# Cross-attention with image-prompt tokens: the output projection one step later with its halves in plain order, and each tile of x loaded in four parts

## What is computed

```python
q = heads(x @ W_q); k_t = heads(text @ W_k); v_t = heads(text @ W_v)
probs_t = softmax(q k_t^T * 32**-0.5)
text_out = probs_t @ v_t
sem = l2norm(probs_t @ text) @ l2norm(ip)^T
probs_ip = softmax(q k_ip^T * 32**-0.5 + 0.5 * sem) * spatial_mask
out = (text_out + probs_ip @ v_ip) @ W_out + b_out + x
```

## Time and profile before

| | |
|---|---|
| times of the kernel before | 1108.41, 1114.44, 1116.14 us (median 1114.44) |
| the profiled execution | 1114.77 us |
| its span from first to last instruction | 1112.9 us |
| granted TensorE clock, mean | 0.974 of full |
| TensorE busy | 92% of the span, over 97% in the middle of the main loop |
| VectorE busy | 76% |
| DMA engines' busy share | 77% |

### The profile page before, as it was taken

One profiled execution on the slowest core, in us unless ns is written; L12 is line 12 of the kernel. 1 busy time (PEld: TensorE's weight loads), 2 busy tenths in 40 slices (PEclk: granted clock), 3 DMA queues, 4 the chain that ended last, 5 costly groups with the idle time before them and its releaser, 6 DMA issues.

```text
span 1112.9 us, 23936 instructions
## 1 busy us (share of the span) xinstructions
PE 1026.0 (92%) x7829; PEld 839.5 (75%) x7829; DVE 840.6 (76%) x2400; ACT 676.1 (61%) x1979; POOL 575.0 (52%) x1535
## 2 busy tenths in 40 slices
PE   6994587899999999999999999999999999999978
PEld 5872466778787878787887878787878787877856
DVE  3145277888888888888888888788878888887862
ACT  1134376766676666766766766676776676676630
POOL 0000255655565665656555656565656656655650
PEclk9798798999999999999999999999999999999989
DMA  9498556877869887968879778878698778877662
GB/s 292 137 210 184 133 112 143 150 161 148 184 130 194 177 166 137 195 136 155 164 159 194 150 161 163 179 138 185 128 199 164 174 146 177 144 143 139 136 115 81
DMA packets 465941, 177.63 MB, mean 160 GB/s; under 512 B 433417, under 2 KB 442917, under 8 KB 465817
## 3 DMA queue, kind: packets, MB, share of 16 engines
q1 hardware_dynamic: 465817, 176.10, 76.6%
HBM read 43.15 MB, written 28.05 MB: 64 GB/s over the span
## 4 chain that ended last, share of the span: by engine, by line
PE 72%; DVE 9%; DMA 4%; issue 2%; POOL 2%; ACT 1%; SPq 1%; DVEq 0%; POOLq 0%
PE ps_O L1003 27%; PE ps_Q L1037 21%; PE ps_U L1023 11%; PE ps_S L979 10%; DMA pts<-ph 3%; PE ps_M L1051 2%; DVE pr L917 1%; DVE n L929 1%; DVE f L933 1%; DVE x_in L866 1%; DVE attn L942 1%; PE ps_M L1065 1%; DVE f L949 1%; DMA x_in<-in_x_dram 1%; ACT pr L770 1%
## 5 line engine op out<-in xcount | busy, mean ns | idle before, releaser
L770 ACT ACTIVATE pr<-ps_S,bias 128x73 f32<-128x73 f32 x1280 | 288.7, 338 | 171.9 <-DVE bias L881 171.9
L847 POOL TENSOR_TENSOR ph<-pr,ph 128x440 f16<-128x440 f32 x320 | 228.2, 734 | 241.2 <-ACT ph L782 241.0
L1003 PE MATMUL ps_O<-wo_hi,aT 128*128 128x320 f16 x1280 | 295.5, 302 | 25.2 <-DVE x_in L866 25.2
L1037 PE MATMUL ps_Q<-xT,wq_hi 128*128 128x512 f32 x800 | 279.7, 415 | 6.2 <-DVE qT L854 6.1
L782 ACT ACTIVATE ph<-pr 128x584 f16<-128x584 f32 x320 | 204.2, 688 | 7.6 <-DMA pts<-ph 2.6
L1003 PE MATMUL ps_O<-wo_lo,aT 128*128 128x320 f16 x640 | 192.2, 300 | 0.0
L1003 PEld LDWEIGHTS ps_O<-wo_hi,aT 128*128 128x128 f16 x1280 | 125.4, 98 | 86.8 <-DVE x_in L866 29.5
L1023 PE MATMUL ps_U<-xm,pts 128*128 128x110 f16 (+1 forms) x2560 | 158.7, 214 | 17.3 <-DMA pts<-ph 16.9
L979 PE MATMUL ps_S<-kbd,qT 128*128 128x308 f32 x960 | 171.0, 314 | 1.1 <-ACT pr L770 1.0
L1037 PEld LDWEIGHTS ps_Q<-xT,wq_hi 128*128 128x128 f32 x800 | 145.9, 190 | 33.5 <-DVE qT L854 8.0
L874 DVE TENSOR_REDUCE smax<-ps_S 128x8 f32<-128x584 f32 x160 | 121.9, 762 | 62.0 <-PE ps_S L979 61.6
(11 more groups left out here) (163 smaller groups left out, 1380.1 us busy)
## 6 DMA issues: line engine op xcount, KB each, us to landing
x_in<-in_x_dram SPq DMA_DIRECT2D x16, 1280.0 KB, 6.7
out_dram<-x_in SPq DMA_DIRECT2D x64, 320.0 KB, 3.1
w_k<-in_L_xattn_W_k_dram SPq DMA_DIRECT2D x5, 512.0 KB, 9.1
w_ip<-in_L_xattn_W_k_ip_dram SPq DMA_DIRECT2D x1, 2560.0 KB, 11.9
w_v<-in_L_xattn_W_v_dram SPq DMA_DIRECT2D x1, 2560.0 KB, 19.8
w_ip<-in_L_xattn_W_v_ip_dram SPq DMA_DIRECT2D x1, 2560.0 KB, 10.3
pts<-ph SPq DMA_TRANSPOSE x160, 4.4
xm<-x_d SPq DMA_DIRECT2D x20, 110.0 KB
```

The costliest lines, as they stand in the source:

```text
L770: last = nc.scalar.activation(pr[p % P_RING][:, j, h, :], sc[:, j, h, 0:T], ACT.Exp, bias=bias[p % 2][:, j, h:h + 1], scale=SCALE)
L847: nc.gpsimd.tensor_tensor(lo, full[:, :, t0:t1], one[:, :, 0, t0:t1], ALU.subtract).then_inc(pl_ready, 1)
L1003: last = nc.tensor.matmul(o_bank[half % 2][:, 0:HALF], stationary, moving, start=(k, a, b_) == O_MMS[0], stop=(k, a, b_) == O_MMS[-1])
L1037: last = nc.tensor.matmul(ps_Q[:], wq[a][:, c, k * P:(k + 1) * P], xT[(CC * i + c) % XT_RING][b_][:], start=(c, a, b_) == Q_MMS[0], stop=( ...
```

## The change

The output of a tile begins in step 6 instead of step 5 after the tile's ten steps, and its pieces go half by half; before, the third pieces of halves 0 and 1 stood together in step 7. The stores and the ring of steps move with it. The load of a tile of x becomes four loads of one subtile (320 KB each), one step after the store that frees the same subtile. In SyncE's order of a step the `pts` transposition now stands before the `aT` transposition, and the load of `vw_sb` is last.

```diff
-    FIRST, LAST = -4, STEPS * (TILES + 1) + 7
+    FIRST, LAST = -4, STEPS * (TILES + 1) + 8
-    OUT_AT = {5: ((0, 0), (0, 1)), 6: ((1, 0), (1, 1)), 7: ((0, 2), (1, 2)), 8: ((2, 0), (2, 1), (2, 2)),
-              9: ((3, 0), (3, 1), (3, 2)), 10: ((4, 0), (4, 1)), 11: ((4, 2), (5, 0)), 12: ((5, 1), (5, 2)),
-              13: ((6, 0), (6, 1), (6, 2)), 14: ((7, 0), (7, 1), (7, 2))}
-    STORE_AT = {9: 0, 11: 1, 14: 2, 16: 3}
+    OUT_AT = {6: ((0, 0), (0, 1)), 7: ((0, 2), (1, 0)), 8: ((1, 1), (1, 2)), 9: ((2, 0), (2, 1), (2, 2)),
+              10: ((3, 0), (3, 1)), 11: ((3, 2), (4, 0)), 12: ((4, 1), (4, 2)), 13: ((5, 0), (5, 1), (5, 2)),
+              14: ((6, 0), (6, 1), (6, 2)), 15: ((7, 0), (7, 1), (7, 2))}
+    OUT_FROM = min(OUT_AT)
+    STORE_AT = {10: 0, 13: 1, 15: 2, 17: 3}
+    LOAD_AT = (-19, -16, -14, -12)
...
                 for j in range(1, TILES):
-                    if p == max(STEPS * j - 13, FIRST):
-                        if j >= X_RING:
-                            sp.wait_ge(x_stored[j % X_RING], 16 * SUB * (j // X_RING))
-                        sp.dma_start(x_in[j % X_RING][:], rows(x, j)).then_inc(x_loaded[j % X_RING], 16)
+                    for q in range(SUB):
+                        if p == max(STEPS * j + LOAD_AT[q], FIRST):
+                            if j >= X_RING:
+                                sp.wait_ge(x_stored[j % X_RING], 16 * (SUB * (j // X_RING - 1) + q + 1))
+                            sp.dma_start(x_in[j % X_RING][:, q], rows(x, j)[:, q]).then_inc(x_loaded[j % X_RING], 16)
...
                     sp.dma_start_transpose(pts[p % PT_RING][:].rearrange("p j k c -> p (j k) c"),
                                            ph[p % PH_RING][:].rearrange("p j h k c -> p (j h k c)")
                                            ).then_inc(pts_loaded[p % PT_RING], 16)
+
+                m = slot_of(p - 5)
+                if m is not None:
+
+                    sp.wait_ge(at_hi, m + 1)
+                    sp.wait_ge(at_lo, m + 1)
+                    if m >= AT_RING:
+                        sp.wait_ge(o_ready, OUTS * ((m - AT_RING) // CC + 1))
+                    sp.dma_start_transpose(aT[m % AT_RING][:], at16[m % 2][:].rearrange("p k s c -> p (k s c)")
+                                           ).then_inc(aT_loaded[m % AT_RING], 16)
+                for b in range(B):
+                    if p == 2 * SLOTS * b + 15:
+
+                        if b:
+                            sp.wait_ge(o_ready, NI * OUTS * b)
+                        else:
+                            sp.dma_start(vw[IPR:IPR + 1].bitcast(F32), b_d).then_inc(vw_loaded, 16)
+                        sp.dma_start(vw[0:IPR].bitcast(F32), vw_d[b]).then_inc(vw_loaded, 16)
...
-                        pe.wait_ge(x_loaded[j % X_RING], 16 * (j // X_RING + 1))
+                        pe.wait_ge(x_loaded[j % X_RING], 16 * (SUB * (j // X_RING + 1) if j % X_RING else SUB * (j // X_RING) + 1))
```

More of the change, by code:

```diff
@@ L646, in out_at @@
     def out_at(p):
-        i, at = divmod(p - 5, STEPS)
-        return [(i - 1, half, piece) for half, piece in OUT_AT[at + 5]] if 0 <= i - 1 < TILES else []
+        i, at = divmod(p - OUT_FROM, STEPS)
+        return [(i - 1, half, piece) for half, piece in OUT_AT[at + OUT_FROM]] if 0 <= i - 1 < TILES else []
     def ip_at(p):
@@ L685, in _ @@
                                              x_d[b, tile, 0:n, c * HG:(c + 1) * HG, :]).then_inc(xm_loaded[c], 16)
[L686 to L692, removed]
+                for i in range(TILES):
+                    if p - STEPS * (i + 1) in STORE_AT:
+                        q = STORE_AT[p - STEPS * (i + 1)]
+                        sp.wait_ge(o_added, OUTS * i + 2 * q + 2)
+                        sp.dma_start(rows(out, i)[:, q], x_in[i % X_RING][:, q, :]).then_inc(x_stored[i % X_RING], 16)
+                for j in range(1, TILES):
+                    for q in range(SUB):
[3 more added lines that the diff above has]
+                            sp.dma_start(x_in[j % X_RING][:, q], rows(x, j)[:, q]).then_inc(x_loaded[j % X_RING], 16)
+                if pair_of(p) is not None:
+                    sp.wait_ge(ph_ready, p + 1)
+                    sp.wait_ge(pl_ready, 2 * (p + 1))
+                    if p >= PT_RING:
+                        sp.wait_ge(u_ready, p - PT_RING + 1)
+                    sp.dma_start_transpose(pts[p % PT_RING][:].rearrange("p j k c -> p (j k) c"),
+                                           ph[p % PH_RING][:].rearrange("p j h k c -> p (j h k c)")
+                                           ).then_inc(pts_loaded[p % PT_RING], 16)
                 m = slot_of(p - 5)
```

## The result

The change made the kernel faster by far less than forecast: 1110.22 us (median of 18 runs, 1101.65 to 1113.97) against 1113.43 (18 runs) for the kernel before, a ratio of 0.9962 with a 95% interval of 0.9948 to 0.9977. Measured again in experiment 1 it was 1109.69 against 1112.50, ratio 0.9969 (0.9950 to 0.9988). That is 3 us off instead of 18.6, and 1110 us lies outside the range of 1086 to 1105.

What follows compares the result with a forecast made beforehand. TensorE was taken to bound the loop, waiting nearly only for VectorE's addition. Terms -20.8 + 2.8 - 5.2 + 1.0 + 0.5 + 5.7 - 1.2 - 1.4 = -18.6 took 1114.77 to 1096 us; range 1086 to 1105.

Steps and rivals of the forecast that it cites:

- the term for `vw_sb`: Load now behind `pts` and `aT` makes TensorE wait in steps 17, 57, 97, 137: +3.0 and +2.7, together +5.7 us.
- The landing: Time from issue to landing of the 400 KB `vw_sb` load, taken as the 3.1 us of a 320 KB DMA.
- The wait in step 8: All 14 loop waits of TensorE for VectorE's addition of a finished half, in step 8 of ten, go: -20.8 us.
- what is late next: Exponentials before the next scores in shortened step 8, and `pts` before U: 0.2 per tile, 14 times, +2.8 us.
- Four loads for one: Load of x in parts: nothing in the loop; first steps -5.2 and +1.0; tile 1's load +0.5 us.
- the blocking rival: Load parts in steps 4, 6 and 8 delay `pts`, TensorE waits 7.8 us per tile: 1205 us, chance 0.05.
- All is hidden: Rival: the `vw_sb` load lands in time and step 8 loses nothing: 1088 us, chance 0.22.
- A new wait takes the place of the old one: Rival: `bias` or `pts`(8) 0.8 to 1.3 us late per tile, 11 to 18 come back: about 1108, chance 0.17.
- Both ends: Step 15, losing 12 output matmuls, counted -1.2 us; the drain counted -1.4 us (from -4 to +2.5).
- The drain's reason: The 2.35 us wait and some 3.8 of VectorE's lateness go, against 2.4 of added matmul work: -1.4 us.

Runs made afterwards that it cites:

- experiment 1: The changed kernel run again unchanged for a second profile, beside the kernel before: 1109.69 us, ratio 0.9969.
- kernel 8: Changed kernel with the `aT` transposition back ahead of the stores and the `vw_sb` load ahead of `pts`: 1091.01 us, repeated at 1091.82.
- kernel 4: Kernel before with only the load of x cut in four parts, output order and SyncE's order as before: 1111.11 us, ratio 0.9980.
- kernel 7: New output order alone: changed kernel with whole loads of x, `aT` at its old place and `vw_sb` ahead of `pts`: 1103.35 us, ratio 0.9907.
- kernel 2: Changed kernel with the `vw_sb` load issued ahead of `pts`, `aT` still behind it: 1095.12 us, repeated at 1092.27.
- kernel 3: Changed kernel with each tile of x loaded whole by one DMA of 1280 KB: 1123.18 us, ratio 1.0093.
- kernel 6: Changed kernel with the `vw_sb` load between `pts` and `aT` instead of behind both: 1098.27 us, ratio 0.9857.
- kernel 5: Kernel before with only SyncE's new order, `aT` behind `pts` and the `vw_sb` load last in its step: 1135.64 us, ratio 1.0200.

## Why the prediction was wrong, step by step

**The ledger of the runs.** New output order alone: -9.6 us (1103.35 against 1112.98). Loads in parts on top of it: -12.3 (1091.01). SyncE's new order on top of both: +18.7 (the changed kernel at 1109.69). Together -3.2, the result, as it must be, since each step is measured from the one before it; the last step crosses two groups of runs. The forecast had the first two right in sum (-24.3 without its term for `vw_sb`, measured -22.0 and -22.2 in the two comparisons of kernel 8) and the third at less than a third of its size. That the first two agree in sum is no proof of their parts: I had put 18.0 on the order and under 4 on the loads, and the order alone gave 9.6. What one is worth depends on the other, as experiments 4 and 7 show.

**The step that failed is the term for `vw_sb`**: +5.7 forecast, +14.6 measured against kernel 2 beside it, +17.4 against its repeat (on another chip). The place (steps 17, 57, 97, 137) was right, and for step 57 the issue time and the deadline to 0.3 us. Two sizes were off.

- *The landing.* I took 3.1 us, the median of a 320 KB store, for a load of 400 KB that stands behind two transposing DMAs and ahead of a load of x. It took 4.3 to 5.0. So the waits were 2.43, 1.93, 1.79 (forecast 1.0 each) and 4.98 (2.7): 11.1 instead of 5.7. Why it took longer is open. The load of x behind it is not the reason: in kernel 3 nothing follows it for 3.7 us in steps 55, 95 and 135, and it releases TensorE 5.0, 4.0 and 4.3 after its issue, against 4.9, 4.4 and 4.3 (rows below; only in step 15 is it 4.2 against 5.0). Nor is `aT` ahead of it alone: in kernel 6 `aT` stands behind it, and the four take 4.0 to 5.5. The bounds that I gave (0 to 9 and 0 to 5) held the waits, 6.2 and 5.0; with the clock behind it the first costs some 7.
- *The clock.* The sum had no term for it, though the trace of before had shown two stretches: one at the wait of 5.28 in its first steps, and one in its drain, behind the 2.35 of the earlier trace rows, where matmuls of O grew from 0.30 to 0.47. Behind some of the waits of 1.6 us and more, and all from 2.9 on, the granted clock was half for 3.4 or 6.8 us. In the changed kernel the three stretches of the loop cost 5.6 and 6.0 us of time in the two profiles (from the steps, as in experiment 5), 1.5 of it behind a `pts` wait; in kernel 5 it was 8.7 for four waits.

Kernel 3's queue and its wait in step 57, with S(55) at 452.41:

```profile
461.22 1.76 SPq L716 DMA_TRANSPOSE aT<-at  x1
463.04 0.57 SPq L725 DMA_DIRECT2D vw_sb<-vw_d  x1
466.79 1.91 SPq L705 DMA_TRANSPOSE pts<-ph  x1
...
467.98 0.42 PE L1005 MATMUL ps_O<-wo_hi,aT 128*128 128x320 f16 x1 [2.62 <-DMA vw_sb<-vw_d]
```

**The wait in step 8 and what is late next: right.** All gaps in the loop went, and with the waits for `vw_sb` gone a tile takes 57.9 to 58.1 us in kernels 2 and 8 (S(28) to S(148) over 12), inside the forecast 57.8 to 58.2. What came in there from S(20) to S(158) is `pts`, 2.3 to 5.1 us, and the exponentials 0.4 once at most: about the 2.8 forecast.

**Four loads for one: right in sign, wrong in where it pays.** Priced at nothing in the loop and -4.2 in the first steps. The first steps gave 5.5 in the profile of kernel 4, and its median under 2 us, for in that profile S(10) to S(148) took 816.3 instead of 812.8. In the loop the parts are worth 12: with the whole load and no gap, `pts` makes TensorE wait up to 3 us, three times in an execution, with half clock at five of those six waits in kernels 3 and 7. The forecast had the cover (the gap of 1.5) in its text on the blocking rival and did not ask what the whole load would have cost without it; since the change makes both edits, the sum did not need the answer. The rule of "DMA: Bandwidth & Descriptors", section Bandwidth, for DMAs of 1 MiB and more is not borne out here as a rule for time. By its section on the anatomy of one DMA, 2.0 us plus bytes over 436 GB/s, a part would take 2.75 us, an estimate; the page fits this to DMAs that GpSimd issues, and these are SyncE's. The parts landed in 3.4 each where the whole took 6.7:

```profile
x_in<-in_x_dram SPq DMA_DIRECT2D x60, 320.0 KB, 3.4
```

Four times 3.4 is twice 6.7, and the kernel was still 12 us faster with them, because what TensorE waits for is the transposition queued behind them (4.4 after its issue behind a part, up to 8.3 behind the whole).

**The rivals.** "All is hidden" (1088) is nearly what kernels 2 and 8 are (1091 to 1095), with `vw_sb` in front. "A new wait takes the place of the old one" had the right outcome, 1108, by the wrong mechanism: it named `bias` and `pts`(8), margins that held, and not the load four times per execution. That case had 0.17. Blocking by the parts did not occur.

**Both ends.** The first ten steps took 60.0 us before and 52.4 and 54.7 in the two profiles of the changed kernel, more off than the 4.2 forecast; the half clock at the wait of 5.28 went with it. The drain's reason was wrong in part: I said that the wait of 2.35 for the addition goes, and waits for it are still there, 3.5 in two and 3.3 in one, only later; the 3.8 of lateness that I counted stood on no row. Its size cannot be judged to the 1.4 us that I gave it: from S(158) on it took 56.6 before, 55.4 and 59.3 in the two profiles of the changed kernel, and windows of 1 us show none and 10 us of half clock in those two.

## What to carry to other kernels

A wait of TensorE is to be priced twice: its length, and up to half of whatever half-clock stretch stands behind it. In this loop, full otherwise, a wait of 1.97 us cost 3.7; the waits of 1.5 had no half clock behind them and cost their length. When a DMA is moved behind others in a queue, take its landing from a load at such a place and not from a store elsewhere, and set it against the deadline in steps; four rare loads took back 15 to 17 of the 22 us that the two other edits had gained. And when two edits belong together, such as closing a gap and cutting the load that the gap covered, each alone tells little: the parts were worth 1.4 us alone and 12 with the gap closed. And where a wait comes in three tiles of fourteen only, compare the queue in those three with the others.

## What the runs showed of the hardware

The granted clock tells short waits apart in a way that I had not expected. In the eleven profiles of the changed kernel and the experiments I looked at every wait of TensorE of 1.5 us or more between 200 and 1030 us. Of those up to 1.56 us none was followed by half clock, nor was any of the gaps in the loop of the kernel before. Of the 17 from 1.60 to 2.62 seven were (1.61, 1.73, 1.93, 1.97, 2.32, 2.40, 2.62) and ten were not (1.60 to 2.57). All 11 from 2.88 to 4.98 were. The stretch began within the wait or up to 1.5 us behind its end, and lasted 3.4 or 6.8 us. A stretch of 3.4 made its steps 1.5 to 1.8 us longer beyond the wait, one of 6.8 2.3 to 3.0. "TensorE: Matmul & The Clock Gate" of the Trainium skill, section "What's actually happening", describes a clock gate that follows how busy the engine has been, with 1.2 and 2.4 GHz as its two levels. The trace agrees with the two levels; which of the waits near 2 us costs a stretch is not to be told from these runs.
